# Gated MLP of two experts: masked rows through both, or rows sorted by expert with indexed DMA

## What is computed

```python
def expert_mask(tt):
    vm = jnp.zeros(tt.shape, dtype=bool)
    vm = vm.at[:, :-1].set((tt[:, :-1] == 1) & (tt[:, 1:] == 1))
    return vm
...
hidden_states = hidden_states + cctx @ cdense_w
mi = rms_norm(hidden_states, ln_post_attn_w)
v_out = jax.nn.silu(mi @ v_gate) * (mi @ v_up) @ v_down
l_out = jax.nn.silu(mi @ l_gate) * (mi @ l_up) @ l_down
hidden_states = hidden_states + jnp.where(vm, v_out, l_out)
return hidden_states
```

## Time and profile before

| | us |
|---|---|
| median of 3 runs | 1402.41 (1401.85 to 1404.24) |
| span of the profiled execution | 1401.6 |
| TensorE matmul busy | 1324.8 (95%) |
| VectorE busy | 869.6 (62%) |
| ScalarE busy | 751.9 (54%) |
| GpSimd busy | 436.4 (31%) |

### The profile page before, as it was taken

The page is one execution under the profiler, slowest core; times in us unless marked ns, Lnnn a source line. Parts: engine busy times, 40 slices in busy tenths (PEclk is TensorE's granted clock), DMA queues, the critical chain, the costliest instruction groups (busy, mean ns, idle before and its releaser), DMA issues.

```text
span 1401.6 us, 32322 instructions
## 1 busy us (share of the span) xinstructions
PE 1324.8 (95%) x10898; PEld 1102.3 (79%) x10898; DVE 869.6 (62%) x1837; ACT 751.9 (54%) x2859; POOL 436.4 (31%) x574
## 2 busy tenths in 40 slices
PE   7978999999997899999899999989989999998999
PEld 6844455555554799999888898889988888987999
DVE  4754566666667776557466666666666656556664
ACT  2323776657767622223866666663367666657422
POOL 1345666557665211000123332211013232323000
PEclk9989999999998999999999999999999999999999
DMA  5230000000000200000100000010001000000000
GB/s 180 79 116 20 5 5 5 0 4 4 4 0 1 98 2 0 0 0 1 65 5 6 4 4 4 1 72 28 0 1 65 6 4 4 7 0 1 9 22 30
DMA packets 13928, 30.33 MB, mean 22 GB/s; under 512 B 2832, under 2 KB 9488, under 8 KB 13200
## 3 DMA queue, kind: packets, MB, share of 16 engines
q1 hardware_dynamic: 13840, 29.23, 6.0%
HBM read 27.13 MB, written 2.10 MB: 21 GB/s over the span
## 4 chain that ended last, share of the span: by engine, by line
PE 73%; POOL 7%; DVE 7%; issue 7%; ACT 5%; POOLq 0%; DVEq 0%; ACTq 0%
PE bank L1029 64%; PE bank L1042 9%; POOL p L2015 2%; ACT p L1795 1%; POOL o L2015 1%; DVE stats L1457 1%; POOL xn L1980 1%; POOL kbd L1996 1%; DVE nmax L1532 1%; DVE pT L1427 1%; POOL kbd L2006 1%; POOL kbd L2015 1%; ACT kbd L1795 0%; DVE w_ff_rounded L1611 0%; POOL rstd L1962 0%
## 5 line engine op out<-in xcount | busy, mean ns | idle before, releaser
L1532 DVE TENSOR_REDUCE nmax<-bank 128x4 f32<-128x512 f32 x256 | 165.3, 684 | 96.0 <-PE bank L1029 94.6
L1029 PE MATMUL bank<-w_ff_rounded,hT_rounded 128*128 128x256 f32 x944 | 217.5, 285 | 4.2 <-ACT w_ff_rounded L1922 3.8
L1795 ACT ACTIVATE p<-bank,nmax 128x128 f32<-128x128 f32 x512 | 181.3, 397 | 70.1 <-DVE nmax L1532 70.0
L1427 DVE COPY pT<-bank 128x512 f32<-128x512 f32 x256 | 164.1, 680 | 88.0 <-PE bank L1042 87.7
L2015 POOL TENSOR_TENSOR p<-p,rshare 128x512 f32<-128x512 f32 x128 | 132.3, 1055 | 217.6 <-DVE rshare L1539 217.6
L1029 PE MATMUL bank<-xT_rounded,w_ff_rounded 128*128 128x256 f32 x864 | 196.3, 285 | 2.0 <-DVE x_all L1647 1.3
L1029 PE MATMUL bank<-xn_rounded,w_ff_rounded 128*128 128x256 f32 x608 | 172.0, 283 | 0.0
L1029 PE MATMUL bank<-xT_rounded,kbd_rounded 128*128 128x256 f32 x608 | 171.9, 283 | 0.0
L1029 PEld LDWEIGHTS bank<-w_ff_rounded,hT_rounded 128*128 128x128 f32 x944 | 163.7, 193 | 5.5 <-issue 4.2
L1029 PEld LDWEIGHTS bank<-xT_rounded,w_ff_rounded 128*128 128x128 f32 x864 | 148.7, 192 | 2.8 <-DVE x_all L1647 1.5
L1732 ACT ACTIVATE o<-bank 128x512 f32<-128x512 f32 (+1 forms) x104 | 60.4, 582 | 164.4 <-PE bank L1029 153.1
(11 more groups left out here) (182 smaller groups left out, 3126.9 us busy)
## 6 DMA issues: line engine op xcount, KB each, us to landing
ctxT<-in_ctxT SPq DMA_DIRECT2D x32, 128.0 KB, 2.4
w_ff<-in_w1b SPq DMA_DIRECT2D x6, 640.0 KB, 6.4
w_att<-in_w2a SPq DMA_DIRECT2D x1, 3072.0 KB
w_att<-in_w3a SPq DMA_DIRECT2D x1, 3072.0 KB
w_att<-in_w1a SPq DMA_DIRECT2D x1, 2304.0 KB
hT<-in_xT SPq DMA_DIRECT2D x8, 256.0 KB, 3.0
o<-in_x SPq DMA_DIRECT2D x8, 256.0 KB, 2.7
w_ff<-in_w2b SPq DMA_DIRECT2D x1, 2048.0 KB, 7.6
```

What stands on the lines that cost most here:

```text
L1029: return pe.matmul(dst, lhsT, rhs, start=first, stop=last)
L1427: dve.tensor_copy(dst, src).then_inc(sems[s[0], "copied"], 1)
L1532: dve.tensor_reduce(nmax[:, s[4], :], bank[:, :].rearrange("p (h t) -> p h t", h=QUAD), AX_X, ALU.max, negate=True).then_inc(sems[s[0], "m ...
L1795: t = act.activation(p[:, part], bank[:, part], ACT.Exp, bias=nmax[:, g, j:j + 1], accum_out=rsum[:, g, j:j + 1])
```

## The change

Rows are sorted by expert before the MLP and each block of 128 goes through one expert.

- After each unit's `end` in phase 1, a new GpSimd step `scatter` writes its two batch rows to a DRAM tensor `x_sorted` with indirect DMAs, row by row to a place looked up in a table `dest`. The table is made once by `index_rows` on GpSimd, ahead of phase 1's loop: the rows of one expert first, those of the other from the next block border on, in each of two halves of 1024 tokens; nine blocks for each half. Counts of earlier rows come from two small matmuls. At the start `x_sorted` is filled with x by four DMAs, so that unused places hold something finite.
- Phase 2 becomes 18 blocks in nine iterations (`MLP_ITERS`) of two. SyncE loads a block, VectorE and GpSimd normalise it, TensorE transposes it (`xT1`). In `gu` the rows are stationary and the weights move, in three thirds of 460, 460 and 456 columns that hold gate and up side by side; the product is transposed (`hT`), and `down` gives rows again, which SyncE stores to `y_sorted`. Which expert's weights move is an offset that TensorE's sequencer reads from a table into a register, once for `gu` and once for `down` of each block.
- In the steps ahead of phase 3 and within its first iteration, 16 indirect DMAs of GpSimd (`gather`) read the results back in token order and add them to x_all.
- `norm_mlp`, the masked copies, the end addition of phase 2, and the weights' 64-row tails go; the weight pieces are 17, in another order, and the straight-line lists of steps ahead of phases 2 and 3 are written anew.

```diff
+EXPERT_PIECES = [0, 1, 2, 3, 4, 5, 8, 9, 10, 6, 7, 11, 12, 13, 16, 14, 15]
+GU_PIECES = EXPERT_PIECES.index(7) + 1
...
-                ([], of_v(("cv", v), ("cq", v)) + keys_c[1:], here(("cdense", u, 1), ("end", u)))]
+                ([], of_v(("cv", v), ("cq", v)) + keys_c[1:], here(("cdense", u, 1), ("end", u), ("scatter", u)))]
...
+    def part(u):
+        v, of_v = (B_, here) if u == A_ else (A_, ahead)
+        return (of_v(("gu", v, 0)) + ahead(("norm_self", u)) + here(("hT", u, 0)) + of_v(("gu", v, 1))
+                + ahead(("scale_mlp", u)) + here(("hT", u, 1)) + ahead(("xT1", u)) + of_v(("gu", v, 2))
+                + here(("down", u)))
+
+    return part(A_) + part(B_)
...
+            def start_of(table, it, u):
+
+                return pe.value_load(table[0:1, bass.ds(it * UNITS + u, 1)], min_val=0, max_val=DC * GU)
...
+            def gu(ph, it, s, bank):
+
+                u, j = s[1:]
+                if j == 0:
+                    pe.wait_ge(*after(ph, it, ("xT1", u), "lo"))
+                    pe.wait_ge(indexed, INDEXED)
+                    if u == A_:
+                        pe.wait_ge(*split(ph, "experts", GU_PIECES - 1))
+                    gu_of[u] = start_of(at_gu, it, u)
+                at, n = THIRDS[j]
+                for c in range(DC):
+                    x, x_lo = (rounded(x_part1(u, low)[:, c * P:(c + 1) * P]) for low in range(2))
+                    part = bass.ds(gu_of[u] + c * GU, GU)
+                    w, w_lo = (t[:, part].rearrange("p (g n) -> p g n", g=2)[:, :, at:at + n] for t in (w_high, w_low))
+                    mm(bank[:, 0:2 * n], x, w, c == 0, False)
+                    mm(bank[:, 0:2 * n], x_lo, w, False, False)
+                    t = mm(bank[:, 0:2 * n], x, w_lo, False, c == DC - 1)
                 t.then_inc(sems[s[0], "mm"], 1)
...
             def down(ph, it, s, bank):
                 u = s[1]
...
+                pe.wait_ge(*after(ph, it, ("hT", u, 1), "lo"))
+                if u == A_:
+                    pe.wait_ge(*split(ph, "experts", len(EXPERT_PIECES) - 1))
+                start = start_of(at_down, it, u)
+                for f in range(F1C):
+                    part = bass.ds(start + (W1B["down0"][0] + f * D), D)
+                    h, h_lo = (rounded(h_part1(u, low)[:, f * P:(f + 1) * P]) for low in range(2))
+                    mm(bank[:, 0:D], h, w_high[:, part], f == 0, False)
+                    mm(bank[:, 0:D], h_lo, w_high[:, part], False, False)
+                    t = mm(bank[:, 0:D], h, w_low[:, part], False, f == F1C - 1)
                 t.then_inc(sems[s[0], "mm"], 1)
...
+            def norm_block(ph, it, s):
+
+                u = s[1]
+                dve.wait_ge(block_in[u], 16 * (it + 1))
+                settle(dve)
+                dve.bn_stats(stats[:, u, 0, :], x_block[u]).then_inc(sems[s[0], "stats"], 1)
+                dve.wait_ge(*after(ph, it, s, "stats"))
+                settle(dve)
+                dve.bn_aggr(aggr[:, u, 0, :], stats[:, u, 0, :]).then_inc(sems[s[0], "aggr"], 1)
...
+            def scale_block(ph, it, s, bank):
+                u = s[1]
+                dve.wait_ge(*after(ph, it, ("norm_self", u), "rstd"))
+                dve.tensor_scalar(x_block[u], x_block[u], rstd[:, u, 0, 0:1], None, ALU.mult).then_inc(sems[s[0], "xn"], 1)
...
+            def gu(ph, it, s, bank):
+                u, j = s[1:]
+                at, n = THIRDS[j]
+                part = hidden[u][:, at:at + n]
+                dve.wait_ge(*after(ph, it, s, "silu"))
+                dve.tensor_tensor(part, bank[:, n:2 * n], part, ALU.mult).then_inc(sems[s[0], "product"], 1)
...
+            def scatter(ph, it, s, bank):
+
+                u = s[1]
+                pool.wait_ge(*after(ph, it, ("end", u), "done"))
+                pool.wait_ge(scattered[u], 16 * ROWS * (it + 1))
+                pool.wait_ge(scattered[1 - u], 16 * ROWS)
...
+                else:
+                    pool.tensor_copy(dest_here[:, u, :], dest[:, rows(it, u)])
+                    pool.tensor_copy(staged[u], x_all[:, rows(it, u), :]).then_inc(staged_done, 1)
+                    pool.wait_ge(staged_done, it * UNITS + (u + 1))
+                    settle(pool)
+                    x_of = [staged[u][:, b, :] for b in range(ROWS)]
+                    to = [dest_here[:, u, b:b + 1] for b in range(ROWS)]
+                for b in range(ROWS):
+                    pool.indirect_dma_start(x_sorted, bass.IndirectOffsetOnAxis(to[b], 0), x_of[b], None)\
+                        .then_inc(scattered[u], 16)
+
+            def gather(ph, it, s, bank):
+
+                row_at = s[1]
+                h = row_at // HALF_ROWS
+                for u in range(UNITS):
+                    pool.wait_ge(y_out[u], 16 + STORES_OF_HALF[h][u])
+                pool.indirect_dma_start(x_all[:, row_at, :], None, y_sorted[h],
+                                        bass.IndirectOffsetOnAxis(dest_in_half[:, row_at:row_at + 1], 0), compute_op=ALU.add)\
+                    .then_inc(y_added[h], 16)
+
+            def index_rows():
+
+                steps = [0]
+
+                def then(t):
+                    t.then_inc(indexed, 1)
+                    steps[0] += 1
+                    pool.wait_ge(indexed, steps[0])
...
```

More of the change, by code:

```diff
@@ L378 @@
     "nT2": "mm wide hi lo", "round": "done", "split": "lo", "finish": "hi", "cq": "mm copied", "ck": "mm flat",
[3 rows of a table removed]
+    "cv": "mm copied", "coT": "copied", "cdense": "mm", "xT1": "mm hi lo", "gu": "mm silu product", "hT": "mm hi lo",
+    "scatter": "", "mrow": "done", "ctx2": "near lo hi", "half": "done", "nT2_low": "",
+    "down": "mm copied", "q2": "mm copied", "k2": "mm copied", "v2": "mm copied", "oT2": "mm hi lo", "oT2_low": "",
     "wo": "mm", "w1": "mm gelu hi lo", "w2": "mm", "end": "done",
@@ L395, in __init__ @@
         self.index = index
+        self.iters = MLP_ITERS if index == 2 else ITERS
         self.layer, self.weave, norm, pre = PLAN[index]
@@ L406, in __init__ @@
         if index == 2:
-            self.once = [("experts", i) for i in range(18)]
+            self.once = [("experts", i) for i in range(len(EXPERT_PIECES))]
         if index in (3, 5):
@@ L425, in __init__ @@
                      for late, kind in enumerate(kinds) if 0 <= i - late < len(self.once)]
+        if index == 3:
+            self.once += [("gather", b) for b in range(B)]
         jobs = [s for s, _ in body if "mm" in EVENTS[s[0]]]
@@ L1261, in down, with turn_hidden @@
+            def turn_hidden(ph, it, s, bank):
+                u, j = s[1:]
+                pe.wait_ge(*after(ph, it, ("gu", u, 2), "product"))
+                starts = [f * P for f in range(QUAD)] if j == 0 else [QUAD * P, TAIL_FROM]
+                turn(s, ph.bank[s], [hidden[u][:, at:at + P] for at in starts])
             def down(ph, it, s, bank):
                 u = s[1]
-                pe.wait_ge(*after(ph, it, ("up1", u, 1, PRODUCTS), "h"))
-                pe.wait_ge(*split(ph, "experts", 17))
@@ new lines, in gu, with turn_hidden @@
+            def gu(ph, it, s, bank):
+                u, j = s[1:]
+                at, n = THIRDS[j]
+                act.wait_ge(*after(ph, it, ("hT", u, 1), "mm", back=1))
+                copy(ph, it, s, hidden[u][:, at:at + n], bank[:, 0:n], event="silu", func=ACT.Silu)
+            def turn_hidden(ph, it, s, bank):
+                u, j = s[1:]
+                part, n = (slice(0, QUAD * P), QUAD * P) if j == 0 else (slice(QUAD * P, F1C * P), (F1C - QUAD) * P)
+                act.wait_ge(*after(ph, it, ("down", u), "mm", back=1))
+                copy(ph, it, s, rounded(h_part1(u, 0)[:, part]), bank[:, 0:n], event="hi")
```

581 lines of the change are left out of this document (290 added, 291 removed), and 3 rows, old and new, of the table EVENTS.

## The result

The changed kernel takes 1457.06 us in the median of 4 runs (1454.0 to 1460.16), the kernel before 1402.6 beside it: a ratio of 1.0386, interval 1.0367 to 1.0404. It is slower by 54 us. The forecast was 1407 (1372 to 1436), slower as the likeliest, so the sign holds and the size doesn't. The profiled execution of after spans 1453.6 us against 1401.6.

A forecast was written before the change was run, and what follows sets the result against it. The prediction took the MLP as TensorE-bound before and bound by the norm's chain after. Its terms, -28 + 0 + 20 + 7 + 2 + 2 + 2 = +5 on 1401.6, gave 1407 us, range 1372 to 1436.

The forecast's parts named there:

- The scatter on POOL: Phase 1's loop: each of six scatters delays TensorE by 3.3 us ahead of scale_self, +20 together.
- The clock: Phase 1: six scatter holes of about 4 us may lower the granted clock, +2 (0 to +10).
- My last part: List of signs; among those of a wrong forecast, a granted clock of 0.5 through the MLP's loop.
- The register reads: MLP blocks: two weight-offset reads by TensorE's sequencer lie beside queued matmuls, 0 (up to +36).
- Rival 3: MLP: the register read sticks out between gu(v,2) and down, 0.8 to 2 us a block, 1420 to 1443; chance 0.28.
- The norm chain: MLP halves: TensorE stands 1.9 us ahead of xT1 for the norm's chain, so a half takes 8.9 us, not 6.9.
- rival 1: MLP: the norm's chain begins early enough and TensorE stays the bound, 32 us back, 1375; chance 0.14.
- The section: MLP, first gate matmul to first query matmul: 174 us against 202, -28 (-24 to -34).
- Block loads have a whole iteration to land in: MLP: SP's block loads and stores have a whole iteration to land in, cost 0.
- the rounding's term: MLP loop's first half: ACT rounds the last six weight pieces ahead of its first silu, estimated 8 us.
- The index: Ahead of phase 1's first in-loop scale_self: 28 small dependent POOL operations, 7.6 us, priced +7 (+3 at the least).
- The way into phase 3: Around phase 3's entry: 16 gathers cost POOL 19 us, mostly beside other work, +2 (0 to 10).

The follow-up runs named there:

- a_pool3: The kernel before with three plain POOL operations, no DMA, ahead of each scale_self in phase 1's loop: 1449.49 us.
- a_pool1: The kernel before with one plain POOL operation, no DMA, ahead of each scale_self in phase 1's loop: 1417.22 us.
- f: The changed kernel with constant weight offsets in gu and down, so no register reads and no choice of expert: 1446.95 us.
- d: The changed kernel with the next block's norm ahead of the first third of gate and up, its scale ahead of the second: 1440.06 us.
- e: The changed kernel with the load of the MLP's third block issued ahead of the 3 MB load of phase 3's weights: 1450.69 us.
- g_index_woven: The changed kernel with its 28 index operations issued two at a time between POOL's other steps ahead of phase 1's loop: 1446.72 us.
- g_gathers: The changed kernel with four gathers in place of eight ahead of phase 3's first norm, the other four behind the second norm: 1456.08 us.
- h_all: The changed kernel with scatters, index operations, filling, block load, norm and first gathers all moved, choice of expert kept: 1380.54 us.

## Why the prediction was right and wrong

- **The scatter on POOL, 3.3 us each: nearly right.** 3.9; the indirect DMA was 1.03 with a gap of 0.30 where I took 1.2, the copy 0.61 where I took 0.6, the wait between them 0.8 where I took 0.15. That POOL's time there is TensorE's time was right, to the tenth: 3.88 us on POOL, 3.88 more of wait.
- **The clock, +2 (0 to +10): the step that failed.** I read from the earlier trace rows that one emptier stretch did no harm and another did, and took the harmless one for the rule. Each of the five scatters' holes in front of the xn transposes costs 3.1 us more in the granted clock, 15.5 together, the hole of the index tables 2.9, and the peeled part runs at 0.73 (462 to 525) where it had 0.88 (412.6 to 470). That is above even my bound of 10. a_pool3 shows the pair of hole and clock without any DMA, a_pool1 the price of the clock alone. My last part looked for a clock of 0.5 in the MLP's loop, where it stayed at 1.00 (558 to 687 us); it was low in phase 1's, for some 7 us after each hole.
- **The register reads, 0 (to +36): wrong.** I covered the read with queued matmuls. f shows 0.75 us a half, 12 us in the loop, though the read is shorter than I took it (0.30 in place of 1.0). What sticks out is mostly the gap before the next block's first matmul. Rival 3 named the cost, and 0.75 is just under the low end of its 0.8 to 2 a block; but it tied it to a read of over 1.2 us, ahead of down, and the read took a quarter of that.
- **The norm chain: right.** 1.9 us of wait predicted, 1.42 measured, of which d gets 1.2 back; rival 1, TensorE as the bound, fell. But the half of 9.21 us agrees with my 8.9 partly because two misses cancel: the chain is shorter than I had it, the reads dearer.
- **The section, -28: -12.8.** Three terms were mis-sized. The halves were 0.3 longer, 16 x 0.3 = 5. The head took 7.5 us (525.84 to 533.32) in place of 2: I had left the first block's own gate and up out of it, 4.5 us ahead of the loop, and a wait of 2.27 for xT1's low part stands behind it. The tail took 27 us (687.84 to 714.90) in place of 22: it has two holes, of 4.83 and 3.56 us, and after the first of them the same matmuls of 256 columns start every 0.215 us until about 705, then every 0.12. The rows:

```profile
701.04 0.55 PE L1024 MATMUL bank<-ctxT_rounded,w_att_rounded 128*128 128x256 f32 x1 [4.83 <-DVE o_rounded L1606]
701.39 0.41 PE L1024 MATMUL bank<-kv_rounded,w_att_rounded 128*128 128x256 f32 x1
701.61 0.41 PE L1024 MATMUL bank<-ctxT_rounded,w_ff_rounded 128*128 128x256 f32 x1
...
706.81 0.28 PE L1024 MATMUL bank<-kv_rounded,w_att_rounded 128*128 128x256 f32 x1
706.93 0.28 PE L1024 MATMUL bank<-ctxT_rounded,w_ff_rounded 128*128 128x256 f32 x1
```

- **"Block loads have a whole iteration to land in: 0": wrong for one.** The first half came out at 16.8 us (533.32 to 550.09) as I had summed it, 8 + 8.9, but by luck: half of its wait was a load behind a 3 MB transfer, and not the rounding. In e the half takes 12.8 (534.80 to 547.64), so the rounding's term was some 4 too large.
- **The index, +7: right for POOL**, 8.4 (the hole of 9.31 against 0.89 before, in the same place); g_index_woven takes it away. The clock behind this hole, 2.9 more, was not in it. The +15.4 of the stretch hides that, because ahead of the index after lost 2.3 less: 44.3 us from phase 0's end to the second scale_self (73.73 to 118.00, clock 0.96) where it was 46.6 (67.53 to 114.14, 0.89), with the same work of POOL.
- **The filling of x_sorted: forgotten, +6.2.** I costed the scatters that write x_sorted and not the DMAs that fill it, though they run beside loads for which TensorE waits.
- **The way into phase 3, +2 for the gathers: +8.6.** I had the last gathers ahead of VectorE's entry into the loop, and priced them too low: of TensorE's holes over 0.4 us, 10.4 us together where before had 3.9, the longest is the 5.17 behind the last gather. The next, 3.95 at 733.28 (1.31 before, 689.70), waits for nothing the profile shows and stays open; g_gathers has it too. The rest is the clock, 0.94 over 714.9 to 813.7 where it was 1.00 (671.7 to 761.9). h_all keeps all of it (+8.4). How much of the +8.6 moving the last gathers would bring back was not run.

The spans differ by 52 us where the sum had 5. Of the 47 between, 16.4 are the clock in phase 1 (18.4 against 2), 15.2 the MLP's, 6.6 the way into phase 3, 6.2 the filling, 3 the scatters' time on POOL (5 x 0.6), 1.2 the stretch ahead of the MLP and 0.6 the index on POOL (46.80 us from the second to the third scale_self, 39.16 before, so 7.6 against 7), less the 2.3 ahead of the index. So the largest term that failed is the clock: a hole ahead of the transposes costs more than its length.

## What to carry to other kernels

Work that was put ahead of an operation for which TensorE already waits was paid nearly in full here, whether it was a plain operation, an indirect DMA or the issuing of plain ones; look for the queue's own slack first, because the same scatter was nearly free 4 to 13 us later, behind scale_self. Where such a hole opens, price the granted clock behind it as well as its length: here it cost four fifths as much again as the hole grew by. A saving in matmul time must be costed together with all that the new loop puts on TensorE's own sequencer, and with its first and last turn, which made two thirds of what the MLP's sum missed here.

## What the runs showed of the hardware

- An indirect DMA of 128 rows of 1 KB holds POOL for 1.03 us (1.54 to 1.6 with an addition), with 0.30 until the next; it lands 2.5 us after its issue (3.8 with the addition). In phase 1's loop the price was the holding; at the entry of phase 3 VectorE waited for a landing.
- The same kind of hole lowered the granted clock or did not: 1.62 us did at 249.8 in a_pool1, 1.97 us at 296.7 did not. All those of 4.1 to 4.8 us in phase 1's loop did, in after and a_pool3, and in after TensorE then ran at 0.50 for 6 to 8 us although it was busy all the time.
- A read of a register from SBUF takes TensorE's sequencer 0.30 us, and yet delays the matmuls behind it: two reads and their addresses cost 0.75 us a block (f_no_register against after).
